# One transformer block with audio cross-attention on one core: banks, order and pieces at the two ends of the audio stage

## The chip, the core and the metric

The kernel runs on one core of a Trainium2 chip. TensorE (PE) multiplies matrices and writes to PSUM, which has eight banks of 512 float32 columns per partition; VectorE (DVE), ScalarE (ACT) and GpSimd (POOL) work element by element; SyncE (SP) issues every DMA of this kernel. Each engine works through its own queue in order, and semaphores tie the queues together. The metric is the device time of one execution in microseconds (us), the median of several.

## The reference, cut to what matters

x is (8, 56, 256), ctx (8, 1500, 256), the mask all ones. The block is

```
for l in (1, 2):                                  # two cross-attentions, 16 heads of 128, plus a bias token
    x = x + cross_attention(layer_norm(x), ctx, ctx, weights of l)
x = x + gelu(layer_norm(x) @ w_fc1 + b_fc1) @ w_fc2 + b_fc2
a = layer_norm(ctx) * gamma + beta                # the audio stage, 16 heads of 16
Q, K, V = heads(x @ Wq.T), heads(a @ Wk.T), heads(a @ Wv.T)
w = softmax(where(mask, Q K^T / 4, -inf))         # 8 x 16 x 56 rows of 1500
out = x + tanh(gate) * (w V merged) @ Wo.T
```

The change touches the third layer norm, the start of the audio stage and its last batch.

## The kernel before, in words

xT holds x transposed, 2 chunks (DC) of 128 features by 448 queries (NQ = 8 batches of 56). Precise products are made of float16 halves, high (by ACT) and low (by DVE), in three passes; products with xT and attnT are plain float32, and each of those matmuls shows in the trace as two records.

**Units.** The keys and values of a batch's 1500 positions are made in 12 units of 128 positions (`unit`, n counts over batches, NT = 12). A unit is 6 matmuls of 512 columns into one bank (`unit_bank`), an ACT op for the high halves (`unit_high`, L1262) and two DVE ops for the low ones (`unit_low`, L1579), which counts m_lo. Sixteen units (PRE_UNITS) are made ahead of the audio loop: units 0 to 7 fill holes in the third layer norm (`LN_UNITS`: 0 to 2, 3 and 4, 5 to 7), unit 8 and 9 to 15 stand between the MLP's products. All sixteen use two banks in turn, M and S[1], so unit n waits for m_lo of n - 2. From unit 16 on three banks are used: TB[0], TB[1], M. Every third unit's keys are turned by a DMA transpose (`turn_keys`, L541). POOL splits the raw context (`split_audio`).

**Queries.** Behind the MLP, 8 float32 products of 448 columns make the queries of all batches, in four windows w of four heads, in PV[0], PV[1], TB[0], TB[1]; ACT (L1384) and DVE (L1757) split them, and for each window DVE spreads batch 0's queries over qbd by four ops (L1762), which counts qbd_ready. POOL does that for later batches (`spread_queries`).

**Tiles.** A batch has 16 x 56 = 896 rows of probabilities, 7 tiles (RT) of 128; y counts tiles over batches, 0 to 55. For a tile PE makes the scores in the three banks S[0..2] (6 matmuls of 512 columns, or 12 where the tile lies in two windows), DVE takes the masked minimum out of PSUM (`audio_minimum`, L1520, as_max), ACT the exponential (L1269), DVE the reciprocal (`audio_scale`, L1527 and L1529), ACT the high halves (`audio_high`, L1278), DVE the low ones (`audio_low`, L1538), and SP turns each of them by one transposing DMA of 12 blocks of 128 x 128 (L550, L552) into probT. PE averages the values per window (`audio_average`, 24 matmuls of 224 columns, into PV[w % 2]), and ACT picks each head's part into attnT by four ops (`pick_average`, L1286, attn_ready).

**The order** is written out by hand, by y: each engine runs its own loop over y, and tables (SLOT_UNITS, SLOT_WINDOWS, SLOT_PICKS, SLOT_KEYS) say which units, averages, picks and key transposes belong to which tile. On PE a slot is scores(y), the first unit of the slot, an average, the other units; scores(y) wait for as_max y, since there is one set of score banks. On ACT it is the high half of y - 1, units, a pick, the exponential of y; on DVE the minimum of y, the low half of y - 1, units, scale(y), units. The last unit belongs to tile 46.

**The end.** Behind tile 55 PE computes the output product of seven batches (EARLY = 392 columns, `early_output`), then the last two averages; DVE adds the seven batches' part to xT (`add_audio`, L1656) behind its last low half, SP writes it out (L619). The last batch's 56 columns follow (L1138), with their addition and output (L622).

## Time and profile before

| | |
|---|---|
| time, median of 3 runs | 1482.26 us (1479.71 to 1484.2) |
| the profiled execution: its own time / its span | 1483.11 us / 1481.2 us |
| PE busy | 1419.8 us, 96% of the span |
| DVE, ACT, POOL busy | 983.6, 867.0, 469.7 us |
| chain that ended last | PE 73%, DVE 8%, DMA 7%, ACT 5%, SP's queue 3% |
| third layer norm, from its means to the MLP | 1099.7 to 1119.0 us |
| MLP, then the queries | 1119.0 to 1150.4, to 1156.5 us |
| audio loop, tiles 0 to 55 (first to last minimum) | 1158.6 to 1464.3 us |
| from the last minimum to the end of the span | 16.9 us |

Times in rows are microseconds from the start of the span. A timeline row has the start, the duration, the engine, the line, the operation, what is written and read, the shape and how many instructions are merged; in brackets stands how long the engine was idle just before and who released it. L755 is the helper that records every matmul, so PE's rows are told apart by their tensors and shapes: `SC<-ctxT` is a unit, `SC<-qc` a tile's scores, `PV<-core` an average.

### The profile page before, as it was taken

How to read it: one execution, taken by the hardware profiler on the slowest of the kernel's cores; microseconds unless marked ns; L12 is line 12 of the kernel's file. 1: busy time of each engine (PE TensorE's matmuls, PEld its weight loads, DVE VectorE, ACT ScalarE, POOL GpSimd, SP SyncE). 2: the span in 40 equal slices, each digit the busy share in tenths (PEclk: the TensorE clock that was granted, in tenths of full speed). 3: DMA queues.
4: the chain of work that ended last, by engine and by line, in shares of the span. 5: the costliest groups of instructions: out<-in, count | busy, mean ns of one | idle time of the engine just before them, and what ended most of it. 6: DMA issues, size and time to landing. Idle time of an engine off the chain costs nothing.

```text
span 1481.2 us, 24729 instructions
## 1 busy us (share of the span) xinstructions
PE 1419.8 (96%) x9188; PEld 891.6 (60%) x9188; DVE 983.6 (66%) x2034; ACT 867.0 (59%) x1564; POOL 469.7 (32%) x379
## 2 busy tenths in 40 slices
PE   8899999999999999999999999999899899999987
PEld 5466666666666654466666666666554455555555
DVE  6665555555556657676566566665557888888886
ACT  5655445544555446545544555445445698888987
POOL 3534425334334200144433433430002333333300
PEclk9999999999999999999999999999999999999999
DMA  5299899898899730398889889988721699999998
GB/s 198 64 228 191 163 185 183 161 187 180 173 177 179 157 102 29 88 205 187 177 171 181 184 164 180 187 164 155 172 58 37 133 218 218 213 210 220 219 201 167
DMA packets 672083, 246.95 MB, mean 167 GB/s; under 512 B 644716, under 2 KB 646236, under 8 KB 671964
## 3 DMA queue, kind: packets, MB, share of 16 engines
q1 hardware_dynamic: 671964, 245.38, 81.6%
q8 instruction: 73, 1.20, 0.3%
q14 instruction: 46, 0.38, 0.1%
HBM read 85.28 MB, written 0.52 MB: 58 GB/s over the span
## 4 chain that ended last, share of the span: by engine, by line
PE 73%; DVE 8%; DMA 7%; ACT 5%; SPq 3%; issue 2%; ACTq 0%; DVEq 0%
PE SC L755 40%; PE PV L755 33%; DMA core<-qc 4%; DVE qc L1538 2%; ACT qc L1278 2%; DVE prob L1520 1%; DMA qc<-core 1%; DVE core L1579 1%; DMA core<-core 1%; ACT prob L1269 1%; SPq L550 1%; ACT core L1262 1%; DVE core L1571 1%; DVE core L1419 1%; DMA core<-in_wv_dram 1%
## 5 line engine op out<-in xcount | busy, mean ns | idle before, releaser
L755 PE MATMUL PV<-core 128*128 128x256 f16 (+1 forms) x4800 | 542.1, 271 | 16.6 <-DMA core<-qc 7.4
L755 PEld LDWEIGHTS PV<-core 128*128 128x128 f16 x4800 | 458.7, 98 | 88.7 <-issue 15.1
L1211 ACT ACTIVATE prob<-SC,core 128x500 f32<-128x500 f32 x336 | 223.8, 674 | 419.5 <-DVE core L1544 419.5
L755 PE MATMUL SC<-ctxT,qc 128*128 128x500 f16 x2016 | 445.4, 375 | 0.0
L1513 DVE TENSOR_REDUCE mx<-SC 128x1 f32<-128x500 f32 x336 | 224.9, 670 | 331.9 <-PE SC L755 331.9
L755 PEld LDWEIGHTS SC<-ctxT,qc 128*128 128x128 f16 x2016 | 196.2, 97 | 208.2 <-issue 1.9
L683 POOL CAST ctxT<-stage 128x750 f16<-128x750 f32 x64 | 69.3, 1083 | 454.9 <-PE SC L755 239.3
L1571 DVE SCALAR_TENSOR_TENSOR core<-prob,core 128x1500 f16<-128x1500 f32 x112 | 194.4, 1736 | 4.3 <-ACT core L1220 4.3
L1220 ACT ACTIVATE core<-prob 128x1500 f16<-128x1500 f32 x112 | 162.7, 1453 | 3.6
L755 PE MATMUL SC<-ctxT 128*128 128x512 f16 x576 | 137.1, 381 | 8.4 <-DVE core L1579 8.3
L755 PE MATMUL SC<-qc 128*128 128x512 f16 x480 | 113.5, 381 | 11.7 <-DVE mx L1520 11.7
L687 POOL TENSOR_TENSOR core<-stage,core 128x768 f16<-128x768 f32 x64 | 109.2, 1706 | 8.6 <-DVE core L1419 3.6
L1538 DVE SCALAR_TENSOR_TENSOR qc<-prob,rsc,qc 128x1500 f16<-128x1500 f32 x56 | 100.2, 1789 | 7.9 <-ACT qc L1278 7.7
L687 POOL TENSOR_TENSOR ctxT<-stage,ctxT 128x750 f16<-128x750 f32 x64 | 101.3, 1583 | 11.6 <-DVE core L1419 6.8
L755 PEld LDWEIGHTS SC<-ctxT 128*128 128x128 f16 x576 | 55.4, 98 | 76.4 <-DVE core L1579 11.8
L1520 DVE CUSTOM_DVE_ANT_0 prob<-SC,rowbuf 128x1500 f32<-128x1500 f32 x56 | 95.9, 1713 | 7.8 <-PE SC L755 7.8
L683 POOL CAST core<-stage 128x768 f16<-128x768 f32 x64 | 56.4, 882 | 136.3 <-DMA stage<-in_ctx_nat_dram 132.6
L1278 ACT ACTIVATE qc<-prob,rsc 128x1500 f16<-128x1500 f32 x56 | 86.2, 1540 | 21.0 <-DMA core<-qc 12.9
L1579 DVE SCALAR_TENSOR_TENSOR core<-SC,rstd,core 128x256 f16<-128x256 f32 x192 | 83.5, 477 | 20.6 <-ACT core L1262 20.6
L705 POOL CAST ctxT<-stage 128x768 f16<-128x768 f32 x32 | 27.0, 842 | 218.6 <-PE SC L755 142.7
L1269 ACT ACTIVATE prob<-prob,mx 128x1500 f32<-128x1500 f32 x56 | 86.5, 1544 | 13.2 <-DVE mx L1520 12.4
L755 PEld LDWEIGHTS SC<-qc 128*128 128x128 f16 x480 | 46.1, 98 | 67.3 <-issue 17.6
(135 smaller groups left out, 1321.5 us busy)
## 6 DMA issues: line engine op xcount, KB each, us to landing
stage<-in_ctx_nat_dram SPq DMA_DIRECT2D x64, 384.0 KB, 3.9
stage<-in_ctx_t_dram SPq DMA_DIRECT2D x64, 375.0 KB, 3.4
stage<-in_ctx_p_dram SPq DMA_DIRECT2D x32, 384.0 KB, 3.9
core<-in_wq_dram SPq DMA_DIRECT2D x8, 512.0 KB, 3.7
core<-in_wk_dram SPq DMA_DIRECT2D x8, 512.0 KB, 3.6
core<-in_wv_dram SPq DMA_DIRECT2D x8, 512.0 KB, 5.1
core<-in_wo_dram SPq DMA_DIRECT2D x8, 512.0 KB, 5.2
core<-core SPq DMA_TRANSPOSE x224, 4.1
```

The source lines that it names most:

```text
L683: nc.gpsimd.tensor_copy(hi, src).then_inc(split_hi, 1)
L687: nc.gpsimd.tensor_tensor(lo, src, hi, ALU.subtract).then_inc(stage_free, 1)
L755: return nc.tensor.matmul(o, a, c, start=start, stop=stop, skip_group_check=skip)
L1211: nc.scalar.activation(prob[:, i, c * CW:c * CW + w], SETS[i][c][:, 0:w], ACT.Exp, bias=nmax[:, i, :], accum_out=sum3[:, i, c:c + 1]).then ...
L1220: nc.scalar.activation(ph[:, i, 0:T], prob[:, i, 0:T], ACT.Copy, scale=UP).then_inc(ph_hi, 1)
L1269: nc.scalar.activation(prob[:, i, 0:T], prob[:, i, 0:T], ACT.Exp, scale=-1.0, bias=mx3[:, i, 0:1], accum_out=sum3[:, i, 0:1]).then_inc(as_ ...
L1278: nc.scalar.activation(aph[:, i, 0:T], prob[:, i, 0:T], ACT.Copy, scale=rsc[:, y % 4, 1:2]).then_inc(aph_hi, 1)
L1513: nc.vector.tensor_reduce(mx3[:, t % 2, c:c + 1], SETS[t % 2][c][:, 0:w], AX_X, ALU.max)\
L1520: nc.vector.tensor_tensor_reduce(out=prob[:, i, 0:T], in0=scores_of(y), in1=maskb[:, b % 2, :], scale=1.0, scalar=3.0e38, op0=ALU.add, op1 ...
L1538: nc.vector.scalar_tensor_tensor(aph[:, i, TC:TC + T], prob[:, i, 0:T], rsc[:, y % 4, 1:2], aph[:, i, 0:T], ALU.mult, ALU.subtract).then_i ...
L1571: nc.vector.scalar_tensor_tensor(ph[:, i, TC:TC + T], prob[:, i, 0:T], UP, ph[:, i, 0:T], ALU.mult, ALU.subtract).then_inc(ph_lo, 1)
L1579: ins = nc.vector.scalar_tensor_tensor(lo[:, i, :, :], src[:, i, :, :], rstd[:, n:n + 1], hi[:, i, :, :], ALU.mult, ALU.subtract)
```

## The change

- Units 0 to 7 go round four banks, M, S[1], PV[0], PV[1], and wait for m_lo of n - 4 only. Units 8 to 15 use the two banks as before. The MLP's first output product, which writes PV[0] and PV[1], waits for the low half of unit 7.
- The queries are made in two parts. Ahead of the loop: batch 0's, 8 products of 56 columns side by side in PV[0], one ACT op and one DVE op of 224 columns. Behind tile 0's scores (`later_queries`, on PE, ACT and DVE): the other seven batches', 8 products of 392 columns in PV[1], TB[0], TB[1], PV[1]; window 3 waits until window 0 is split (aq_lo 2), and unit 16 waits until all are (aq_lo 5). On ACT and DVE this part stands behind the exponential and the scale of tile 0.
- The last batch's scores alternate between the banks S[0..2] and TB[0], TB[1], M, and wait for the minimum of the tile before last.
- The early output has six batches (336 columns) and stands in PE's queue behind tile 47's scores, its additions in DVE's behind the low half of tile 47, its DMAs in SP's ahead of tile 49's transposes. Tile 49's scores wait for the additions. The final part has 112 columns.
- The last tile's high and low halves are made in two pieces each (768 and 732 columns), and turned by four transposes of 6 blocks each.

```
-EARLY = (B - 1) * Q
+EARLY = (B - 2) * Q
+LATER = (B - 1) * Q
+ALONE = RT * (B - 1)
...
         def unit_bank(n, y):
 
+            if n < FIRST_MLP_UNIT:
+                return (M, S[1], PV[0][:, :], PV[1][:, :])[n % 4]
...
+            return NB * 512 if y >= ALONE and (y - ALONE) % 2 == 0 else 0
...
+        QUERY_BANKS = (PV[1], TB[0], TB[1], PV[1])
+        HALVES = ((0, NT // 2 * P), (NT // 2 * P, T))
...
+            def turn_last():
+
+                y, s, i = RT * B - 1, RT - 1, (RT * B - 1) % 2
+                half = NT // 2
+                sp.wait_ge(apv_done, NW * (B - 2) + LAST_WINDOW[s] + 1)
+                for n, lo in ((0, 0), (1, 0), (0, NT), (1, NT)):
+                    sp.wait_ge(aph_lo if lo else aph_hi, y + n + 1)
+                    j = lo + n * half
+                    sp.dma_start_transpose(probT[:, j:j + half, s * P:(s + 1) * P], aph[:, i, j * P:(j + half) * P])\
+                        .then_inc(half_full[1 if lo else 0] if n else (aptl_full if lo else apth_full)[i], 16)
+
             for y in range(RT * B + 1):
                 b, s = divmod(y, RT)
+                if y == ALONE + 1:
+                    early_out()
...
-                if n < PRE_UNITS and n >= 2:
+                if 4 <= n < FIRST_MLP_UNIT:
+                    pe.wait_ge(m_lo, n - 3)
+                if FIRST_MLP_UNIT <= n < PRE_UNITS:
                     pe.wait_ge(m_lo, n - 1)
                 if n == PRE_UNITS:
                     pe.wait_ge(m_lo, PRE_UNITS)
-                    pe.wait_ge(aq_lo, NW)
+                    pe.wait_ge(aq_lo, 1 + NW)
...
+                elif y < ALONE:
+                    pe.wait_ge(as_max, y)
                 else:
-                    pe.wait_ge(as_max, y)
+                    pe.wait_ge(as_max, y - 1)
+                if y == ALONE:
+                    pe.wait_ge(y_ready, DC)
...
+            def later_queries():
+
+                for w in range(NW):
+                    if w == NW - 1:
+                        pe.wait_ge(aq_lo, 2)
+                    for c in range(DC):
+                        ins = mm(QUERY_BANKS[w][:, 0:LATER], wqa[:, c, w, :], xT[:, c, Q:NQ], c == 0, c == DC - 1)
+                    ins.then_inc(aq_mm, 1)
...
                     if y < RT * B:
                         audio_scores(y)
+                    if y == 0:
+                        later_queries()
...
-                    if y == RT * B:
+                    if y == ALONE - 2:
                         for m in range(DC):
                             early_output(m)
...
+                    if f == 0:
+                        pe.wait_ge(m_lo, FIRST_MLP_UNIT)
...
-            banks = PV + TB
             for w in range(NW):
                 for c in range(DC):
                     pe.wait_ge(x_ready, 2 * DC + c + 1)
-                    ins = mm(banks[w][:, 0:NQ], wqa[:, c, w, :], xT[:, c, :], c == 0, c == DC - 1)
-                ins.then_inc(aq_mm, 1)
+                    ins = mm(PV[0][:, w * Q:(w + 1) * Q], wqa[:, c, w, :], xT[:, c, 0:Q], c == 0, c == DC - 1)
+            ins.then_inc(aq_mm, 1)
...
+                if y == ALONE - 1:
                     add_audio(TB, ew_mm, 0, EARLY)
```

## Rows read from the trace of the kernel before

**Rows 1.** Page, part 1: busy us (share of the span) x instructions.

```profile
PE 1419.8 (96%) x9188; PEld 891.6 (60%) x9188; DVE 983.6 (66%) x2034; ACT 867.0 (59%) x1564; POOL 469.7 (32%) x379
```

**Rows 2.** Windows: length, busy per engine, PE clock, DMA share, GB/s; MLP, audio loop.

```profile
1120.00:1140.00 20.00, 19.62 (x99) 9.33 (x97) 15.22 (x32) 11.96 (x19) 5.68 (x4) 0.98 0.21 40
...
1200.00:1300.00 100.00, 94.64 (x564) 53.71 (x564) 87.93 (x157) 89.82 (x130) 40.26 (x32) 1.00 1.13 218
```

**Rows 3.** Timeline, third layer norm: unit 2, low halves 5 and 6, units 7 and 8.

```profile
1104.82 1.47 PE L755 MATMUL SC<-ctxT 128*128 128x512 f16 x6 [0.75 <-DVE core L1579]
...
1115.93 1.65 DVE L1579 SCALAR_TENSOR_TENSOR core<-SC,rstd,core 128x256 f16<-128x256 f32 x4
1116.84 0.33 PEld L755 LDWEIGHTS SC<-ctxT 128*128 128x128 f16 x3 [3.48 <-DVE core L1579]
1116.85 2.41 PE L755 MATMUL SC<-ctxT 128*128 128x512 f16 x6 [2.99 <-DVE core L1579]
...
1122.10 1.46 PE L755 MATMUL SC<-ctxT 128*128 128x512 f16 x6
```

**Rows 4.** Windows behind that stall.

```profile
1118.85:1120.90 2.05, 2.05 (x7) 0.85 (x6) 0.88 (x2) 1.59 (x2) 0.00 (x0) 0.56 0.57 106
1120.90:1122.90 2.00, 2.00 (x12) 0.97 (x10) 0.82 (x2) 1.99 (x5) 0.00 (x0) 1.00 0.00 0
```

**Rows 5.** Timeline: queries, spreads, tile 0 and tile 1.

```profile
1150.45 3.25 PE L755 MATMUL PV<-xT,ctxT 128*128 128x448 f32 x8 [0.83 <-DVE xT L1752]
...
1152.23 0.54 ACT L1384 ACTIVATE qc<-PV 128x448 f16<-128x448 f32 x1 [1.76 <-PE PV L755]
...
1153.47 0.73 DVE L1762 TENSOR_SCALAR qc<-qc,hm 128x112 f16<-128x112 f16 x4
...
1156.54 1.46 PE L755 MATMUL SC<-qc 128*128 128x512 f16 x6
...
1160.37 1.54 ACT L1269 ACTIVATE prob<-prob,mx 128x1500 f32<-128x1500 f32 x1 [3.09 <-DVE mx L1520]
...
1160.67 2.75 PE L755 MATMUL SC<-qc 128*128 128x512 f16 x12
...
1163.46 1.72 DVE L1520 CUSTOM_DVE_ANT_0 prob<-SC,rowbuf 128x1500 f32<-128x1500 f32 x1
```

**Rows 6.** Timeline of PE alone: tile 48's scores, an average, tile 50's scores.

```profile
1430.73 2.25 PE L755 MATMUL SC<-qc 128*128 128x512 f16 x6 [2.40 <-DVE mx L1520]
1432.77 3.40 PE L755 MATMUL PV<-core 128*128 128x224 f16 x24
...
1439.49 0.81 PE L755 MATMUL SC<-qc 128*128 128x512 f16 x3 [2.02 <-DVE mx L1520]
```

**Rows 7.** Timeline, last batch, ACT: high half of tile 48, pick, exponential of tile 54.

```profile
1437.24 1.54 ACT L1278 ACTIVATE qc<-prob,rsc 128x1500 f16<-128x1500 f32 x1 [0.58 <-DVE rsc L1529]
1438.81 1.23 ACT L1286 ACTIVATE small<-PV,vbias 32x56 f32<-32x56 f32 x4
...
1462.38 1.54 ACT L1269 ACTIVATE prob<-prob,mx 128x1500 f32<-128x1500 f32 x1
```

**Rows 8.** Timeline of the end: early output, its additions, last average, final products.

```profile
1465.87 5.44 PE L755 MATMUL SC<-small,ctxT 128*128 128x392 f32 x16
...
1471.41 1.16 DVE L1656 SCALAR_TENSOR_TENSOR xT<-SC,tg,xT 128x392 f32<-128x392 f32 x2
...
1475.43 1.31 PE L755 MATMUL PV<-core 128*128 128x224 f16 x12 [0.48 <-DMA core<-qc]
...
1476.58 2.13 PE L755 MATMUL SC<-small,ctxT 128*128 128x56 f32 x16
```

**Rows 9.** By line, ns min/median/max: transposes of 4 blocks (L518), of 12 (L552, last three).

```profile
L518 SPq DMA_TRANSPOSE qc<-core x112: 1188/1237/2170, 95.0 to 1056.9; - x112
...
DMA to landing us min/median/max: 2.4/2.5/4.6
...
L552 SPq DMA_TRANSPOSE core<-qc x3: 1450/1454/1473, 1463.8 to 1471.5; - x3
...
DMA to landing us min/median/max: 3.8/3.8/3.9
```

## What I expect of it, written ahead of the result

> **What bounds the kernel now.** I read the page first, for which engine is full, then the timeline at the places that the diff touches, then the waits, and the windows view for the stretches between. TensorE (PE) is busy 96% of the span [rows 1]. In the MLP it is busy 19.62 of 20 us and in the audio loop 94.64 of 100, where VectorE (DVE) has 87.93, ScalarE (ACT) 89.82 and the DMA share is 1.13 [rows 2]: nobody has room, so a delay at the loop's start is handed on. In the last batch, which has no units left, PE waits for as_max and the loop ACT, DVE, ACT sets the pace [rows 7]. All times below are of the profiled execution: span 1481.2 us, own time 1483.11, which is 0.85 above the median of the three runs (1482.26). I work out a difference and put it on the median.
>
> **1. Four banks for units 0 to 7.** Today unit 2 waits 0.75 us for the low half of unit 0, and unit 7 waits 2.99 us for that of unit 5; after that unit 7 runs at half speed, 2.41 us for 6 matmuls [rows 3]. The granted clock is still 0.56 up to 1120.90, and full (1.00) in the next stretch [rows 4]. With four banks unit 2 follows unit 1 at once, and the whole norm moves 0.75 us forward: DVE's low halves of units 5 and 6 began at 1115.93 and took 1.65 us together [rows 3], so they end at 1115.93 + 1.65 - 0.75 = 1116.83. PE meanwhile has units 5 to 7 without a gap and at the full clock: 12 matmuls of 512 columns take 2.75 with their run-out [rows 5], so 1.28 a unit; unit 6 ended at 1116.85 - 2.99 = 1113.86, unit 5 began at 1111.1, now at 1110.35, and unit 7 ends at 1114.2. The two first MLP products follow (the last two matmuls of the first wait for h_ready, which comes as DVE turns to unit 5's low half, 1115.2), and PE stands at unit 8 by 1116.75. Unit 8 still waits for unit 6's low half, 1116.85 plus a semaphore: 1117.0, where it began at 1122.10 [rows 3]. **-5.1 us.** The new wait ahead of the first output product (unit 7 low, some 1117.8) is over before that product is due at 1119.4; queued behind it are only PE's later products. The MLP hands it on, for PE was busy 98% there. Bounds: -5.4 if unit 8 follows PE alone, -3.9 if DVE, with ACT's Gelu table load between, runs each low half a whole unit late.
>
> **2. Batch 0's queries apart.** Today 8 products of 448 columns keep PE from 1150.45 to the scores of tile 0 at 1156.54, so 6.1 us; tile 1's scores start at 1160.67 [rows 5]. Afterwards 8 products of 56 columns: 16 records took 2.13 us, a short wait included [rows 8], so some 1.9, and they end at 1152.6, for the second half of xT comes some half a microsecond behind the first. One ACT copy of 224 columns (0.54 for 448 [rows 5], so 0.33) and one DVE op (0.4) lead to 1153.6; the first four spreads take 0.73 [rows 5], so tile 0's scores start at 1154.45, 2.1 early. The other twelve spreads hold DVE to 1156.6, where tile 0's minimum starts, 2.0 early. But then later_queries stands in PE's queue ahead of units 16 and 17 and tile 1's scores. At 392 columns 16 records took 5.44 us, 0.34 each [rows 8]: windows 0 to 2 run from 1155.75 to 1159.8. Window 3 reuses PV1 and waits for aq_lo 2, and ACT makes window 0's high half only behind tile 0's exponential. That one was at 1160.37, it comes 2.0 earlier, 1158.37, and takes 1.54 [rows 5] and 0.1 of read-out; ACT copy 0.49, DVE 0.58 [rows 8]: 1161.2. Window 3 ends at 1162.6, its two halves at 1163.9, and unit 16 waits for exactly that (aq_lo 5). Units 16 and 17 take 2.6: tile 1's scores start at **1166.5 instead of 1160.67, +5.8 us**, and its minimum at 1169.25 instead of 1163.46 [rows 5]. From there DVE's queue is the same as before, and it was full. Bounds: +3.1 with both waits gone (PE's own work, 1.9 + 5.4 against 6.1, and the wait for the first spread, 1.9); +6.3 if the later halves run half a microsecond late. I take +5.8, since every piece has a row.
>
> **3. Six batches' output ahead.** It leaves the slot after tile 55, where it cost nothing: tile 55's last 12 matmuls waited 0.48 us for their transposed halves, long behind it [rows 8]. It goes behind tile 47's scores. There PE idles 2.40 us and then runs tile 48's scores at the low clock, 2.25 us for 6 matmuls [rows 6]. 336 columns cost 5.44 x 336 / 392 = 4.66 us: 1428.4 (1430.73 - 2.40) to 1433.05. Tile 48's scores then run at the full clock (1.46) and end at 1434.5 against 1432.98: +1.5. DVE has minimum, low half of tile 47 and now the two additions (1.16 for two of 392 columns [rows 8], so 1.0) ahead of scale(48): it ends at 1439.35, and ACT's high half of tile 48, at 1437.24 before [rows 6], starts 2.1 later. Tile 49's scores wait for y_ready: 1439.05, while PE was through at 1436.75 (24 matmuls of the average, 2.4 at the full clock, behind them). That gap, 2.3 us, lies between one of 2.02 that kept the clock and one of 2.40 that lost it [rows 6]. Kept: tile 49's exponential starts 2.2 late; lost: the scores take 2.25 and it is 3.1. I take the middle, **+2.65**. Bounds: +1.4 (only tile 48's scores late) and +3.4. The output DMAs hold SP some 1.4 us ahead of tile 49's transposes, which no engine waits for then: 0.
>
> **4. Two bank sets.** Here the price is small. PE's waits for as_max go, but between them stands ACT: high half, pick (1.23), exponential [rows 7]. Tile 54's exponential starts at 1462.38 with no idle time of ACT ahead of it, behind a pick [rows 7]; an earlier minimum buys nothing. Only tile 50's minimum, 0.19 late through PE, comes forward: **-0.2** (0 to -0.4).
>
> **5. Last tile in halves.** ACT's two halves (0.85, 0.81) start at 1468.13, DVE's end at 1470.9 against 1471.5: -0.6. But SP issues four transposes for two. One of 12 blocks takes SP 1.45 us and lands 3.8 us after its start; one of 4 blocks still takes 1.19 to 1.24 and lands in 2.5 [rows 9]. For 6 blocks that is 1.25 and 2.8: issued at 1469.0, 1470.3, 1471.5, 1472.8, the last lands at 1475.6 against 1475.3. **+0.3** (-0.6 if a half takes SP 0.85; +0.6). The final products have 112 columns for 56: +0.1.
>
> The Trainium skill (DMA: Bandwidth & Descriptors, Rules for kernel authors) speaks against such halves: many small transfers should be made one large one. The trace agrees as far as SP goes [rows 9]. With no price on the split this part would be -0.6 and the sum +2.7; by the rule, as by the rows, it is +0.3 and +3.6.
>
> **Tail clock.** With the early output gone, PE has nothing between the average that ends by some 1464.3 and tile 54's turned high half, some 1469.9. After 2.99 idle the clock was low for some 4 us [rows 3, 4]. Here it would be full again at 1473.9, ahead of the last matmuls: 0, at worst +0.8 (12 matmuls of 224 columns at half speed, 1.31 more, less the waits they cover).
>
> **Sum:** -5.1 + 5.8 + 2.65 - 0.2 + 0.3 + 0.1 = **+3.6 us**: 1484.8 of span, **1485.8** on the median. Bounds added up: -5.4 + 3.1 + 1.4 - 0.4 - 0.6 = -1.9, and -3.9 + 6.3 + 3.4 + 0.7 + 0.8 = +7.3.
>
> **Rivals.** (a) The loop takes up part of tile 1's delay. For it: DMA is the fullest thing in the loop, and tile 0's high half reaches SP only 3.3 us late. Against: it was idle between the first two transposes anyhow. Part 2 is then +3.3, the sum +1.1: 1483.4. (b) Faster: the loop's pace comes from the transposes alone and both added delays (parts 2 and 3) vanish in their queue, while part 1, which moves the first transpose too, stays: -5.1 + 0.1 = -5.0: 1477.3. Against it: ACT, DVE and PE each stand near 90% [rows 2]. (c) Slower: the clock. The gap ahead of tile 49 loses it (+3.1, from a gap between 2.02 and 2.40 on), and TensorE stays low through the last average (+0.8), with part 1 at -4.5: +3.6 + 0.45 + 0.8 + 0.6 = +5.45: 1487.7. For it: two of the three gaps named above did it. The Trainium skill (TensorE: Matmul & The Clock Gate, HAM oscillation) has this as a pattern: where waits part groups of matmuls, each group starts at the low clock. The trace agrees for gaps of 2.40 and 2.99, not for 2.02. (d) The banks don't do it: the stall of unit 7 goes, but unit 8 or the first output product waits as long, part 1 gives -1.0: +7.7: 1490.
>
> **How the numbers follow.** Forecast 0.45; in a third of it (tile 49 at the low clock and a little more) the difference passes 0.3%, 4.4 us, about what a measurement here can tell from no change. (a) 0.17, (b) 0.13, (c) 0.20, (d) 0.05. Faster 0.13; same 0.30 + 0.17 = 0.47; slower 0.15 + 0.20 + 0.05 = 0.40. The range leaves out (b) and (d), 0.18, and goes from (a) with its terms at their best, some -2.7, to the added upper bounds: 1479.5 to 1489.5. The likeliest's own range is 1484 to 1487.
>
> **What would show it.** Right: no PE idle ahead of unit 7, unit 8 starting 5.1 earlier; PE waiting twice between tile 0's and tile 1's scores, with 12 us between their starts (4.13 before); ACT's high half of tile 48 some 2 late within its batch; four SP issues of 1.25 at the end. Wrong: loop periods that differ by more than 0.2 us a batch, or a last batch whose exponentials come closer together than 3.7 and 4.9.

## The result, and the profile after

The changed kernel takes **1487.95 us** (median, 1485.93 to 1489.86), the one before beside it 1481.64 (1479.71 to 1486.08). The ratio is 1.0036, with a 95% interval of 1.0023 to 1.005: 5.3 us slower (3.4 to 7.4). The forecast was 1485.8, a difference of +3.6. That lies inside the interval and the time inside the range, but I had called "within 0.3%" the likelier class, and it came out as slower by over 0.3%, by a little. Of the numbers that I had named, the nearest to the time is 1487.7, that of rival (c).

The profiled execution of after has a span of 1486.6 us, against 1481.2. From its page, part 1:

```profile
PE 1425.5 (96%) x9204; PEld 897.7 (60%) x9204; DVE 987.0 (66%) x2036; ACT 867.5 (58%) x1566; POOL 469.9 (32%) x379
```

TensorE has 5.7 us more of busy time than in [rows 1], with 16 records more (the eight later products of the queries). Still 96%: the page shows no new bottleneck, and the difference has to be looked for place by place. For this I cut every execution at the same instructions: the third norm's first mean product (the anchor, where the two programs have done the same work), then the starts of the audio tiles' minimum, the custom operation on VectorE. Every number of this table is the difference of two starts in a timeline:

| us | before | after | after minus before |
|---|---|---|---|
| start to anchor | 1099.71 | 1099.46 | -0.25 |
| anchor to tile 0's minimum | 58.91 | 52.09 | -6.82 |
| to tile 1's | 4.84 | 12.68 | +7.84 |
| to tile 47's (the loop) | 265.41 | 265.37 | -0.04 |
| to tile 49's | 8.74 | 11.89 | +3.15 |
| to tile 53's | 18.13 | 17.16 | -0.97 |
| to tile 55's | 8.58 | 9.63 | +1.05 |
| to the end | 16.88 | 18.32 | +1.44 |

The sum is +5.4, the whole difference of the spans. Now the places, from the timeline of after (start, length, engine, line, operation, count, [idle before it and its releaser]). First the third norm, units 5 to 8 on TensorE, the first two MLP products between:

```profile
1111.21 2.75 PE L788 MATMUL PV<-ctxT 128*128 128x512 f16 x12
...
1113.81 2.65 PE L788 MATMUL SC<-core 128*128 128x448 f16 x12
...
1116.45 1.47 PE L788 MATMUL SC<-ctxT 128*128 128x512 f16 x6
```

No idle time is left where [rows 3] have 2.99 us ahead of unit 7, and unit 8 starts at 1116.45 against 1122.10: 5.65 earlier, 5.4 of it since the anchor. Then the queries:

```profile
1144.81 2.21 PE L788 MATMUL PV<-xT,ctxT 128*128 128x56 f32 x16 [0.83 <-DVE xT L1847]
...
1148.65 2.74 PE L788 MATMUL SC<-qc 128*128 128x512 f16 x6 [1.64 <-DVE qc L1856]
...
1151.55 1.72 DVE L1595 CUSTOM_DVE_ANT_0 prob<-SC,rowbuf 128x1500 f32<-128x1500 f32 x1 [1.05 <-PE SC L788]
...
1155.99 1.58 PE L788 MATMUL PV<-xT,ctxT 128*128 128x392 f32 x4 [0.32 <-DVE qc L1747]
1158.85 2.75 PE L788 MATMUL SC<-ctxT 128*128 128x512 f16 x12 [1.28 <-DVE qc L1747]
1161.44 2.75 PE L788 MATMUL SC<-qc 128*128 128x512 f16 x12
1164.23 1.72 DVE L1595 CUSTOM_DVE_ANT_0 prob<-SC,rowbuf 128x1500 f32<-128x1500 f32 x1 [2.29 <-PE SC L788]
```

The batch's own queries are quick, but tile 0's scores take 2.74 us where they took 1.46 [rows 5]. TensorE waits twice behind them, 0.32 and 1.28, ahead of the fourth window's products and of units 16 and 17. The scores of tile 1 start 12.8 us behind those of tile 0. The windows (length, busy by engine, granted clock, DMA share, GB/s) of the gap ahead of tile 0's scores, and of the scores:

```profile
1147.00:1148.60 1.60, 0.02 (x1) 0.00 (x0) 1.12 (x6) 0.36 (x1) 0.00 (x0) 0.97 0.00 0
1148.65:1151.19 2.54, 2.54 (x7) 1.07 (x7) 1.85 (x12) 0.00 (x0) 0.00 (x0) 0.50 0.00 0
```

The low one of the two levels, 1.2 GHz, holds over the whole of tile 0's scores. Now the last batch: early output products, tile 48's scores, the additions, tile 49's scores, exponential, and what SyncE issues behind tile 50.

```profile
1429.21 4.76 PE L788 MATMUL SC<-small,ctxT 128*128 128x336 f32 x16
1433.81 1.46 PE L788 MATMUL SC<-qc 128*128 128x512 f16 x6
...
1438.64 1.03 DVE L1740 SCALAR_TENSOR_TENSOR xT<-SC,tg,xT 128x336 f32<-128x336 f32 x2
...
1439.89 4.04 PE L788 MATMUL SC<-qc 128*128 128x512 f16 x18 [2.32 <-issue]
...
1446.72 1.07 SPq L550 DMA_DIRECT2D out_dram<-xT  x2
...
1452.17 2.45 SPq L569 DMA_TRANSPOSE core<-qc  x1
1454.67 1.89 SPq L571 DMA_TRANSPOSE core<-qc  x1
...
1457.27 1.31 PE L788 MATMUL PV<-core 128*128 128x224 f16 x12 [3.20 <-DMA core<-qc]
1458.95 2.29 PE L788 MATMUL PV<-core 128*128 128x224 f16 x12 [0.37 <-DMA core<-qc]
1461.03 4.80 PE L788 MATMUL SC<-qc 128*128 128x512 f16 x18
```

Two things are as forecast here: the early output takes 4.76 us (4.66 worked out), and the wait for y_ready leaves a gap of 2.32 that, in this execution, keeps the clock (the 18 matmuls of tiles 49 and 50 in 4.04 are at full speed). One isn't: an average waits 3.20 us for a transposed half, behind SyncE's writes. And behind that wait the clock falls, in the stretch in which the second half of the average is made:

```profile
1458.95:1461.00 2.05, 2.05 (x12) 1.67 (x13) 2.05 (x3) 1.96 (x2) 0.00 (x0) 0.54 1.14 212
```

So that half takes 2.29 us and the 18 matmuls of tiles 54 and 55 take 4.80, where the same work takes 1.33 and 4.05 in a kernel that keeps the clock here (writes_late, below): 1.7 us more ahead of tile 54's minimum, which waits 2.15 us for TensorE. Last, the end:

```profile
1473.34 5.57 SPq L634 DMA_TRANSPOSE core<-qc  x4
...
1473.83 6.41 PE L788 MATMUL PV<-core 128*128 128x224 f16 x36 [5.70 <-DMA core<-qc]
...
1480.57 1.31 PE L788 MATMUL PV<-core 128*128 128x224 f16 x12 [0.34 <-DMA core<-qc]
1481.73 2.18 PE L788 MATMUL SC<-small,ctxT 128*128 128x112 f32 x16
```

TensorE comes out of 5.70 us of idle time, runs its 36 matmuls in 6.41 us (the granted clock is 0.50 up to 1478), and then still waits 0.34 for the last half.

### The profile page after: what moved, and what is told of

Same layout as the page of the kernel before. It is cut to its first block, busy times and chain, and to the rows that moved or that the text cites. A ratio compares the mean times of both kernels' runs of the same rounds, so it can differ in the third digit from the quotient of the medians.

```text
span 1486.6 us, 24770 instructions
## 1 busy us (share of the span) xinstructions
PE 1425.5 (96%) x9204; PEld 897.7 (60%) x9204; DVE 987.0 (66%) x2036; ACT 867.5 (58%) x1566; POOL 469.9 (32%) x379
## 4 chain that ended last, share of the span: by engine, by line
PE 73%; DVE 8%; DMA 8%; ACT 5%; issue 3%; SPq 3%; ACTq 0%; DVEq 0%
PE SC L788 39%; PE PV L788 33%; DMA core<-qc 3%; DVE qc L1622 2%; DMA qc<-core 2%; DVE prob L1595 1%; DMA core<-core 1%; ACT qc L1343 1%; DVE core L1663 1%; ACT prob L1325 1%; ACT core L1318 1%; DVE core L1655 1%; DVE core L1494 1%; ACT small L1351 1%; DVE prob L1499 1%
## 5 line engine op out<-in xcount | busy, mean ns | idle before, releaser
L788 PE MATMUL SC<-ctxT 128*128 128x512 f16 x552 | 130.6, 379 | 5.5 <-DVE core L1663 4.2
L1663 DVE SCALAR_TENSOR_TENSOR core<-SC,rstd,core 128x256 f16<-128x256 f32 x184 | 80.0, 477 | 14.8 <-ACT core L1318 14.8
```

Of the source, the lines that this page charges most:

```text
L788: return nc.tensor.matmul(o, a, c, start=start, stop=stop, skip_group_check=skip)
L1663: ins = nc.vector.scalar_tensor_tensor(lo[:, i, :, :], src[:, i, :, :], rstd[:, n:n + 1], hi[:, i, :, :], ALU.mult, ALU.subtract)
```

## The experiments

**How far one execution can be trusted.** The kernel before was run twice more, unchanged.

> The kernel before once more, for a second profile. From tile 1's to tile 47's minimum it took 265.4 us, and the nine changed kernels 265.4 to 269.6, though they differ nowhere in that stretch. My theory: this is the loop's own scatter between executions (transposes that land late or in time), so further profiles of the kernel before lie anywhere from 265 to 269. Rival (an earlier start makes the loop longer, by 2 us on average, and so eats part of the four banks' gain): 265.0 to 265.8 again.

> The kernel before a third time, for the same question: theory 265 to 269 us from tile 1's to tile 47's minimum, rival 265.0 to 265.8.

The stretch from tile 1's to tile 47's minimum took 268.08 and 265.31 us, where it had taken 265.41. Of the other pieces of the table the start to the anchor (1097.91 and 1095.38 against 1099.71) and the end (17.22 and 17.41 against 16.88) differ too; the rest agree with the first execution within 0.03 us. So the unchanged kernel's loop scatters by 2.8 us, though only one of the two new executions shows it. Over all fourteen profiled executions the loop took 265.3 to 269.6, and the anchor stood at 1095.0 to 1100.5 in programs that are the same up to there. A single time, or a span, can't judge an edit of 1 us. The pieces outside the loop are steadier, but not fixed. Where the code up to there is that of the changed kernel, tile 1's minimum stands 64.7 or 64.8 behind the anchor in five kernels and 64.29 in a sixth (writes_late); and where the stretch around tile 49 is that of the changed kernel, it took 11.89 from tile 47's to tile 49's minimum in five kernels and 12.26, 12.89 and 12.82 in three. An effect below 1 us that one execution shows is therefore not shown.

From tile 1's to tile 3's minimum it took 9.95 or 9.96 us in every kernel, so a delay of tile 1 isn't caught up there. Nor is it later: the three kernels that reach tile 1 5.4 us sooner than before, measured from the anchor (58.4), have loops of 266.2, 267.9 and 266.9, the eleven others 267.0 on average.

**The banks alone.** Kernel before, with the four banks:

```diff
+            if n < FIRST_MLP_UNIT:
+                return (M, S[1], PV[0][:, :], PV[1][:, :])[n % 4]
...
-                if n < PRE_UNITS and n >= 2:
+                if 4 <= n < FIRST_MLP_UNIT:
+                    pe.wait_ge(m_lo, n - 3)
+                if FIRST_MLP_UNIT <= n < PRE_UNITS:
                     pe.wait_ge(m_lo, n - 1)
...
+                    if f == 0:
+                        pe.wait_ge(m_lo, FIRST_MLP_UNIT)
```

> The kernel before with part 1 alone (four banks for units 0 to 7 and the wait ahead of the first output product). My theory: part 1 is worth what the trace of the changed kernel shows up to the queries, 5.4 us, and the audio loop hands it on: unit 8 starts 5.4 us earlier, every minimum from tile 0 to tile 55 some 5.4 earlier, time 5.4 below before. Rival (the loop's pace swallows shifts at its start): unit 8 earlier by 5.4, but tile 55's minimum by 2 or less, and the time less than 2.5 below before.

From the anchor to tile 0's minimum it took 53.54 instead of 58.91: -5.37, and tile 1's followed after 4.85 as before (4.84). Timed: 1478.3 us, ratio 0.9975 (0.9959 to 0.9991), so -3.7 us (-6.1 to -1.3), an interval that holds the 5.4. The gain is real, and most of it is handed on. The profiled execution gives less than the theory at tile 55, whose minimum stands 3.3 us earlier behind the anchor, not 5.4: its loop took 0.8 more than before's first execution, and its last batch 1.25 more (36.70 against 35.45), in code that the edit doesn't touch. There tile 50's scores came behind a gap of 3.21 us at the low clock, 4.44 us for 12 matmuls. The rival asked for 2 or less there and for less than 2.5 in the time; the first is out, the interval of the second reaches down to 1.3.

**Banks and two score sets**, the early output at its old place:

```diff
+            return NB * 512 if y >= ALONE and (y - ALONE) % 2 == 1 else 0
...
-                    pe.wait_ge(as_max, y)
+                    pe.wait_ge(as_max, y if y <= ALONE else y - 1)
...
                 pe.wait_ge(attn_ready, NW * (B - 1))
+                pe.wait_ge(as_max, RT * B - 1)
```

> Part 1 and two bank sets in the last batch, with the early output where it was before; tile 49 stays on the old set, tile 50 takes the other one, and so on, so that the early output's banks are free one tile earlier. It is the version that keeps only what I hold to be gains. My theory: 5.4 from part 1 and 0.3 to 0.5 more from the last batch, so 5.7 to 5.9 below before, and nothing that waits longer. Rival: PE running ahead in the last batch is itself what cost time there, since it then idles, loses the clock and meets later averages cold: no gain over part 1 alone, or up to 1 us worse.

From tile 47's to tile 55's minimum: 35.18 against 35.45, so -0.27; the end 16.92 against 16.88. Timed: 1478.68 us, ratio 0.997 (0.9959 to 0.998): -4.4 us (-6.1 to -3.0). The 0.27 lies at tile 50's minimum, 4.40 behind tile 49's instead of 4.67, where part 4 of the prediction had its 0.2; I had expected 5.7 to 5.9 in all, and the interval just reaches that. **This version beats both kernels**, and so does banks_alone. What the sets add to the banks can't be told in the time (1478.68 and 1478.3), only in the profile.

**The queries back together**, in the changed kernel: the four 448-column products, with later_queries called by no engine.

```diff
-                    ins = mm(PV[0][:, w * Q:(w + 1) * Q], wqa[:, c, w, :], xT[:, c, 0:Q], c == 0, c == DC - 1)
-            ins.then_inc(aq_mm, 1)
+                    ins = mm(banks[w][:, 0:NQ], wqa[:, c, w, :], xT[:, c, :], c == 0, c == DC - 1)
+                ins.then_inc(aq_mm, 1)
```

> The changed kernel with part 2 undone: all queries ahead of the loop in four banks. My theory: tile 1's minimum comes 6.4 us earlier than in the changed kernel and the loop hands that on, so the time is 6.4 us (5.4 to 7.4) below the changed kernel, about equal to before. Rival (the loop absorbs a late tile 1 through its transposes): less than 3.5 below the changed kernel.

```profile
1146.47 1.46 PE L788 MATMUL SC<-qc 128*128 128x512 f16 x6
1148.02 2.75 PE L788 MATMUL SC<-ctxT 128*128 128x512 f16 x12
```

Its timeline shows TensorE without a gap between the scores of tile 0 and of tile 1. Tile 1's minimum stands 58.37 us behind the anchor, where it is 64.77 in the changed kernel: 6.40. Timed: 1482.03 us, ratio 1.0002 (0.999 to 1.0013), which is 3.4 thousandths, 5.0 us, below the changed kernel's ratio (some 2.4 to 7.6, from the two intervals). Part 2 is the largest loss, and it arrives at the end. The times alone would not exclude the rival's 3.5; the lengths of the loops speak against it.

**The gap ahead of tile 0's scores filled**, in the changed kernel, with seven products (14 records) that nobody reads:

```diff
             ins.then_inc(aq_mm, 1)
+            keep_clock(7)
             audio_attention()
```

> The changed kernel with seven 128-column matmuls in the gap ahead of tile 0's scores, which the changed kernel runs at the low clock (granted 0.50). My theory: the clock falls for lack of work around that gap, and it is the 0.6 us by which part 2 cost more than I had worked out: with the gap filled tile 0's scores take 1.46 and not 2.74, tile 0's minimum comes 1.0 earlier and tile 1's 0.6 to 1.0 earlier. Rival (the low clock there has been set by the light products of 56 columns ahead of the gap, too early for a filler to help): the scores still take over 2.2 and tile 1's minimum stays within 0.3.

```profile
1143.08 2.21 PE L788 MATMUL PV<-xT,ctxT 128*128 128x56 f32 x16 [0.83 <-DVE xT L1848]
1145.13 1.79 PE L788 MATMUL SC<-dmean 128*128 128x128 f32 x14
1146.93 1.47 PE L788 MATMUL SC<-qc 128*128 128x512 f16 x6
```

With the gap covered, the scores take 1.47 us, not 2.74. Tile 0's minimum comes 50.96 behind the anchor instead of 52.09, and tile 1's still 12.67 after it: 1.13 us for both, and the granted clock is 1.00 over the scores. So a gap without work in it is what lets the clock fall here, and the fall costs 1.1. Where in the scores it comes differs between executions: in writes_late, whose code is the same up to there, they take 2.23 us and both minimums come 0.5 earlier than in the changed kernel. The whole time (1490.09, 8.85 above the kernel before beside it) is of no use: the loop took 269.64 here, the longest of all.

**The waits for the fourth window's bank gone**, in the changed kernel, and the later queries ahead of tile 0's exponential and scale:

```diff
-        QUERY_BANKS = (PV[1], TB[0], TB[1], PV[1])
+        QUERY_BANKS = (PV[1], TB[0], TB[1], M)
...
-                    if w == NW - 1:
-                        pe.wait_ge(aq_lo, 2)
...
+                    if y == 0:
+                        later_queries()
                     if b < B:
                         audio_exponentiate(y)
-                    if y == 0:
-                        later_queries()
```

> The changed kernel with the later queries in four banks (no wait for window 0's halves) and their halves ahead of tile 0's exponential on ScalarE and ahead of its scale on VectorE. My theory: of the 6.4 us that part 2 costs at tile 1, the two waits are the smaller part, and TensorE's own products and the wait for the first spreads the larger: unit 16 starts 1.0 to 1.5 earlier than in the changed kernel, and tile 1's minimum as much. Rival (the two waits of 1.3 us each and what hangs on them are the cost, as their 2.6 us would say): 2.6 or more earlier.

```profile
1146.73 2.19 PE L788 MATMUL SC<-qc 128*128 128x512 f16 x6 [1.64 <-DVE qc L1854]
...
1148.72 2.49 PE L788 MATMUL PV<-xT,ctxT 128*128 128x392 f32 x4
...
1156.43 2.75 PE L788 MATMUL SC<-ctxT 128*128 128x512 f16 x12 [1.28 <-DVE qc L1745]
```

A miss for both theories. Tile 1's minimum stands 64.28 behind the anchor against 64.77. But writes_late, without this edit, has 64.29, so nothing shows that the edit brought anything. Of the two waits only the first, 0.32, is gone. The one ahead of unit 16 stayed at 1.28: it is the hand-over of the last pair of halves, behind whichever product comes last. Tile 0's scores and the first four records still pay the low clock, here in other shares (2.19 and 2.49 us, against 2.74 and 1.85 in the changed kernel), 4.5 and 4.4 us in all from the first start to the last end. And where gap_filled has the full clock, the fourth window's wait grows from 0.32 to 0.77: the low clock had covered a part of it. What is left of part 2 here, 64.28 less 58.39, so 5.9, is for one half idle time of TensorE that stayed (1.64 for the first spread, 1.28 for the last halves); the low clock is 1.1 of the other, and the rest, some 1.9 by difference, TensorE's additional work. This order of the other engines took none of it away.

**The early output back behind tile 55**, with seven batches again, in the changed kernel:

```diff
-EARLY = (B - 2) * Q
+EARLY = (B - 1) * Q
...
-                if y == ALONE:
-                    pe.wait_ge(y_ready, DC)
...
-                    if y == ALONE - 2:
+                    if y == RT * B:
```

> The changed kernel with the early output, its additions and its writes back behind tile 55, for seven batches, and no wait for them ahead of tile 49. My theory: part 3 costs 2.45 through the additions and tile 49's wait, and 1.06 more through the writes that hold up SP's transposes (tile 54 waits for the first average, which waits for tile 50's transposes): the time is 3.5 us below the changed kernel, the exponential of tile 49 comes 2.4 earlier, and TensorE does not idle 3.2 us ahead of the last batch's first average. The last average keeps the full clock. Rival (the 1.06 comes from PE running ahead on two bank sets and going cold, not from the writes): only 2.5 below, with tile 54's minimum still waiting for PE.

From tile 47's to tile 55's minimum it took 35.17 instead of 38.68: 3.5 us back. Of these 2.45 lie between tiles 47 and 53 (26.60 for 29.05) and 1.05 between 53 and 55. But the end stayed at 18.24 (18.32). Its timeline, and a window in it:

```profile
1470.08 7.34 PE L787 MATMUL SC<-small,ctxT 128*128 128x392 f32 x16 [0.60 <-issue]
...
1477.26 4.78 PE L787 MATMUL PV<-core 128*128 128x224 f16 x48
```

```profile
1470.00:1472.00 2.00, 1.92 (x3) 1.18 (x4) 1.97 (x3) 1.64 (x2) 0.00 (x0) 0.50 0.48 95
```

The early output ran at the low clock for its first part, 7.34 us where [rows 8] have 5.44, and all 48 matmuls of two averages stand behind it. Here TensorE is what ends last, not the transposes. The timed ratio, 1.0025 (1.0012 to 1.0039), lies only 1.6 us below that of the changed kernel, and the two intervals overlap; the expected 3.5 is neither confirmed nor excluded by the times. In the profiled execution the loop took 267.86, 2.5 us more than in that of the changed kernel.

**Only the writes of the early output moved**, behind SyncE's last transpose:

```diff
-                if y == ALONE + 1:
-                    early_out()
...
+            early_out()
             for c in range(DC):
                 sp.wait_ge(y_ready, DC + c + 1)
```

> The changed kernel, with only the writes of the early output moved in SP's queue, from ahead of tile 49's transposes to behind those of tile 55. My theory: the two writes hold SP and the DMA engines when the transposes of tiles 49 and 50 are due; without them the first average of the last batch no longer waits 3.2 us for tile 50's halves, tile 54's minimum comes right behind tile 53's chain (exponentials 4.9 apart or less, not 5.9), and the end is 1.1 us earlier. Rival (running ahead on two bank sets, TensorE going cold): the 3.2 us wait and the late tile 54 are still there.

```profile
1455.04 1.74 SPq L569 DMA_TRANSPOSE core<-qc  x1
1455.69 1.31 PE L787 MATMUL PV<-core 128*128 128x224 f16 x12 [1.17 <-DMA core<-qc]
1456.85 1.77 SPq L571 DMA_TRANSPOSE core<-qc  x1
1457.32 1.33 PE L787 MATMUL PV<-core 128*128 128x224 f16 x12 [0.32 <-DMA core<-qc]
```

The average waits 1.17 instead of 3.20, the clock stays at 1.00, and from tile 53's to tile 55's minimum it is 8.58 again, not 9.63: the expected 1.05. From tile 47's minimum on the gain is only 0.57 (38.11 against 38.68), for in this execution the clock fell behind the gap ahead of tile 49, ahead of everything that the edit touches. SyncE issues back to back from 1446.72 to past 1465 in the changed kernel, and the two writes are 1.07 of it.

The rival, TensorE going cold, isn't disposed of by this: both happen at the same place. Over all kernels: of seven that have the writes there, five took 9.6 to 11.3 on this piece and two (queries_first and whole_warm) 8.6; of seven that don't, all took 8.6. And in exactly those five the granted clock is low behind the two waits, so that the average's second half takes 2.20 to 2.42 us and not 1.31 to 1.33; in the two others and in writes_late it stays at 1.00. In the five the two waits add up to 3.6 to 4.3 us, in the three to 1.5 to 2.9. So late transposes alone didn't delay tile 54's minimum; a delay came where the clock fell as well. Worked out for the changed kernel, the 1.7 us of the low clock are more than the whole delay of 1.05. The writes are a likely cause of the long waits, not a certain one: the single issue of 3.3 or 3.5 us that precedes the wait in queries_whole, gap_filled and last_whole has its like in every kernel. Each of the fourteen executions, before's three too, has 28 to 35 single transposes in the audio stage whose issue takes over 2.3 us.

**The last tile whole**, in the changed kernel:

```diff
-                if y == RT * B:
-                    turn_last()
-                elif y > 0:
+                if y > 0:
                     turn_audio(y - 1)
...
-                    if n == NW * B - 1:
-                        pe.wait_ge(half_full[i], 16)
```

> The changed kernel with the last tile's halves and transposes whole again. My theory: four issues of 1.28 us in a row cost more than the earlier start gives; the low half then lands some 3.95 later than in the kernel before, and the last average's second half starts 1.1 to 1.2 us earlier relative to tile 55's scale than in the changed kernel. Rival (the low clock behind the 5.7 us idle gap is what makes the tail longer): the last average's second half starts no more than 0.3 earlier.

```profile
1477.81 1.43 SPq L569 DMA_TRANSPOSE core<-qc  x1
1477.97 7.58 PE L786 MATMUL PV<-core 128*128 128x224 f16 x48 [5.67 <-issue]
1479.62 1.51 SPq L571 DMA_TRANSPOSE core<-qc  x1
```

```profile
1478.00:1480.00 2.00, 2.00 (x12) 1.62 (x13) 1.60 (x1) 1.00 (x4) 0.00 (x0) 0.50 1.14 213
1480.00:1482.00 2.00, 2.00 (x12) 1.65 (x11) 0.00 (x0) 0.00 (x0) 0.00 (x0) 0.50 1.13 211
1482.00:1484.00 2.00, 2.00 (x14) 1.66 (x12) 0.00 (x0) 1.19 (x4) 0.00 (x0) 0.55 0.45 83
```

The end takes 17.77 instead of 18.32, so the halves cost 0.55 as the end stands, half of what I expected. The other half may be hidden by the clock: issued at 1479.62 and landing 3.7 us later, the last half is there at 1483.4, but the 48 matmuls run without a gap until 1485.5, at 0.50 up to 1482 and still mostly low up to 1484 (0.55). At the full clock the last 12 (1.31) would have ended at 1484.75. That 0.8 is worked out, not shown. Two kernels were to show it.

**The tail kept warm**, with the last tile whole and in halves: 20 products that nobody reads, in tile 56's slot.

```diff
+                    if y == RT * B:
+                        pe.wait_ge(as_max, RT * B - 1)
+                        for _ in range(20):
+                            mm(S[1][:, 0:P], dmean[:, :], dmean[:, :], True, True)
```

> The kernel last_whole (the changed kernel with the last tile whole) plus 20 matmuls of 128 columns behind tile 55's scores and the average there, ahead of the last two averages, whose products nobody reads. last_whole took 17.77 us from the last minimum to the end of the span, where the kernel before took 16.88. My theory: the rest is the low clock (granted 0.50 for 5.7 us), since TensorE comes to the last second half late; with it kept busy the tail takes 16.9 to 17.1. Rival (the 112 columns instead of 56 and what follows them are the rest): 17.5 or more.

> The changed kernel plus the same 20 matmuls. My theory: with the last tile in halves the fourth transpose lands so late that the clock has time to come back, so the tail stays at 18.2 to 18.4 us, and the split by itself costs 1.2 to 1.4 us against whole_warm. Rival (the low clock is what costs here too): 17.5 or less.

Neither bore out the theory. With the last tile whole the clock did stay at 1.00, but tile 55's high half landed only 5.1 us after its issue, SyncE needed 2.71 us to issue the low one, and DMA moved 41 GB/s meanwhile:

```profile
1475.72 2.71 SPq L571 DMA_TRANSPOSE core<-qc  x1
...
1479.17 2.61 PE L786 MATMUL PV<-core 128*128 128x224 f16 x24 [1.97 <-DMA core<-qc]
```

```profile
1476.00:1478.00 2.00, 1.21 (x12) 0.95 (x10) 0.00 (x0) 0.73 (x3) 0.00 (x0) 1.00 1.15 41
```

The end took 17.87, which is what the rival asked for (17.5 or more), but a landing 1.3 us later than the usual 3.8 is enough to explain it. In halves, the four issues took 1280 to 2114 ns each, TensorE waited 2.43 and then ran at 0.50 for two more microseconds, and the end took 19.17, outside both ranges. The difference of the two, 1.30, is the 1.2 to 1.4 that I had expected for the split, but with a slow transfer in each it shows little. An issue of 2.71 us isn't peculiar to the fillers, as said above; whether they make one likelier, no run shows. How the end's cost divides between clock and halves stays open.

## Why the prediction was right or wrong, point by point

| us | forecast | measured | from |
|---|---|---|---|
| 1. four banks | -5.1 | -5.37 | banks_alone |
| 2. queries apart | +5.8 | +6.4 | after less banks_alone: 64.77 - 58.39 |
| 3. output ahead | +2.65 | +2.45 | after less output_back, tiles 47 to 53 |
| its writes, with the low clock there | 0 | +1.05 | after less writes_late, tiles 53 to 55 |
| 4. two sets | -0.2 | -0.27 | banks_and_sets less before |
| 5. halves, clock, 112 columns | +0.4 | +1.4 | the end: 18.32 - 16.88 |
| sum | +3.6 | +5.7 | in the profiled pair, with -0.3 from the rest: +5.4 |

The total was right by its range only: the three large misses (0.6, 1.05 and 1.0) all lie on the slow side. Each entry from a single pair of executions can be off by up to 1 us, by the scatter above. And the -2.7 at the lower end of my range follows from none of my terms; the lower bounds add up to -1.9. It decided nothing here.

**1 was right**, with its mechanism: no wait ahead of unit 7, a full clock, unit 8 as soon as VectorE has given a bank back. My 5.1 let unit 8 wait for unit 6's low half until 1117.0, a start it beat by 0.3.

**2 had the right mechanism and a term too small.** The two waits behind tile 0 stand where I put them, unit 16's at 1.28 where I had 1.3, the fourth window's at only 0.32 where my times gave 1.4 (1159.8 to 1161.2). What I missed was ahead of them: I ran tile 0's scores "2.1 early" with the 1.46 of [rows 5]. They did start 2.3 earlier since the anchor, beyond part 1, but stood behind a gap of 1.64 that ended at the low clock, and took 2.74. I had looked for the clock at the gaps that already existed and not at the one that this part makes. gap_filled puts 1.13 on it. Against that the scores started 0.2 earlier than I had them, and the fourth window's wait, 0.77 even at the full clock, was shorter than allowed, so the term is off by 0.6 in all.

The Trainium skill (TensorE: Matmul & The Clock Gate, What's actually happening) ties the clock to how busy the engine has been of late. The traces agree as far as filling the gap with work kept the clock (gap_filled). They show no more exact rule: 1.64 us of idle time behind the 56-column products lost it every time, but 2.32 us behind one and the same work, ahead of tile 49, kept it in five executions and lost it in three:

```profile
1442.55:1444.50 1.95, 1.95 (x6) 0.77 (x7) 0.02 (x1) 1.85 (x3) 0.00 (x0) 0.57 1.13 210
```

This is last_whole, in the first 2 us of tile 49's scores, where the changed kernel has 1.00; nothing differs in its code up to there.

**3 was right in place and size.** The additions and the wait for y_ready did it. I had put 2.2 on the case that the gap keeps the clock, 3.1 on the other, and had taken the middle. The changed kernel's execution is the first case, with 2.45. Over the eight executions with this early output, from tile 47's to tile 53's minimum, the mean is 29.35, 2.75 above output_back: both cases occur, and the middle was the right thing to take. **The failed step is "the output DMAs hold SP some 1.4 us ahead of tile 49's transposes, which no engine waits for then: 0".** That looked at the transposes next in line. The queue stays full behind them. In all likelihood the 1.07 comes out at an average ahead of tile 54's scores, where the wait, 3.20 us, then loses the clock too: 1.05 us in the changed kernel, nothing in two other kernels that have the writes at the same place.

**4 was right**, -0.27 for -0.2: ScalarE sets the pace there [rows 7].

**5 failed in size.** The rows that I scaled held (1.28 us for an issue and 2.8 to land, where I had 1.25 and 2.8), but the sequence started late and ran long:

```profile
L634 SPq DMA_TRANSPOSE core<-qc x4: 1279/1284/1576, 1473.3 to 1477.6; - x4
...
DMA to landing us min/median/max: 2.8/2.8/3.1
```

By line, in ns min/median/max, with the first and last start. Counted from tile 55's minimum, I had the first issue at 4.7 and the last at 8.5; they came at 5.1 and 9.3, since SyncE was still issuing tile 54's low half, 1.46 us from 1471.78 on, and the first of the four took 1.58. The last half was used 12.3 behind the minimum and 11.1 before. The remaining 0.26 are the wider final products, where I had 0.1. The "tail clock: 0" was right for this kernel by 0.34 us only, the wait that TensorE still had: the clock was back not 4 us after the restart but past 1479, over 5 us after it. The +1.4 is against before's best end: those of all kernels with the old end lie at 16.9 to 17.5, those in halves, the warmed one aside, at 18.24 to 18.32.

Here the Trainium skill (DMA: Bandwidth & Descriptors, Issuing engines are not separate DMA queues) calls the sequencer time of starting a transfer usually small relative to the transfer. The rows differ: 1.28 of issue for 2.8 to landing, and issues stand in line.

**The rivals.** (a), the loop takes up some of tile 1's delay, 2.5 us of it: not seen, by the 9.95 us that no kernel shortens and by loops that are as long behind an early tile 1 as behind a late one; queries_whole's 5.0 us alone, with its wide interval, would not exclude it. (b), faster: out; both delays arrive. (c), the clock: its 1487.7 came nearest to the 1487.95, and that is partly luck. The low clock did cost, but 1.1 ahead of tile 0's scores and its part of the 1.05 ahead of tile 54's, neither of which I had; at the gap ahead of tile 49, where I placed it, it came in three of eight executions and not in the profiled one of the changed kernel, and at the end of the changed kernel nothing shows that it cost time, since TensorE, slow as it was, still waited 0.34 for the last half. (d), banks without effect: out. What took the result over 0.3% are the two terms of SyncE, which I had at 0 and 0.3, and the clock ahead of tile 0: bounded from above with a full queue and a low clock, they would have made slower the likelier class.

## What to carry to other kernels

Work moved out of a slot that a landing transfer covers must be paid where it goes, and each instruction of it counts: here the products, the additions behind another engine's wait, and probably 1.07 us of writes in a queue of transposes. Look for the clock at the gaps that a change makes, not only at those that are there. Splitting a hand-over to start the first part sooner pays only if the rest isn't ahead of the next item in an in-order queue: tile 0 came 1.5 us sooner by it and tile 1, which sets the pace, 6.4 later. Take the change apart before judging it: a few free banks for filler units were worth 5.4 us, more than all the rest could hope for, and the versions that keep these, with the second score set or without (1478.7 and 1478.3 us, not to be told apart), are the ones to use.

## What the runs showed of the hardware

- The granted clock fell to 0.50 behind a gap of 1.64 us after sixteen 56-column records, each time; seven products in that gap kept it at 1.00. A gap of 2.02 [rows 6] kept it. One of 2.32 behind the same code kept it in five executions and lost it in three. A gap's length alone doesn't tell.
- The low clock and a wait behind it cover each other: at the full clock the fourth window waited 0.77, not 0.32.
- A transpose's issue has a part that doesn't shrink: 1.28 us for 6 blocks, 1.45 for 12 [rows 9]. In the audio stage some 30 single issues of each execution took over 2.3 us, up to 4.3, in the kernel before as in the others.
- Identical loop code took 265.3 to 269.6 us over 46 tiles from one execution to the next, more than most edits here are worth.
